# Scores of the first three query blocks with the keys held in 128x32 tiles and turned back by VectorE

## The reference

```python
q = jnp.concatenate([q_nope, apply_rope(q_rope)], axis=-1)
...
scores = jnp.einsum('bqhd,bkhd->bhqk', q, k) * scale
mask = jnp.tril(jnp.ones((S, S), dtype=bool))
scores = jnp.where(mask, scores, jnp.finfo(scores.dtype).min)
attn = jax.nn.softmax(scores, axis=-1)
out = jnp.einsum('bhqk,bkhd->bqhd', attn, v).reshape(B, S, N_HEADS * V_DIM)
return out @ Wo
```

## Time and profile before

| | us |
|---|---|
| median of 3 runs | 819.32 (818.69 to 820.13) |
| the profiled execution | 820.57 |
| its span from first to last instruction | 818.7 |
| TensorE busy | 800.7 (98%) |
| VectorE busy | 666.7 (81%) |
| ScalarE busy | 522.1 (64%) |
| GpSimd busy | 468.0 (57%) |

### The profile page before, as it was taken

How to read it: one execution, slowest core, us unless ns; L and a number is a source line. 1 busy time by engine, 2 the same in 40 slices (tenths; PEclk the granted TensorE clock), 3 DMA queues, 4 the chain that set the end, 5 groups by cost and what they waited for, 6 DMA issues and landing times.

```text
span 818.7 us, 22149 instructions
## 1 busy us (share of the span) xinstructions
PE 800.7 (98%) x7528; PEld 738.5 (90%) x7528; DVE 666.7 (81%) x2509; ACT 522.1 (64%) x1612; POOL 468.0 (57%) x1245
## 2 busy tenths in 40 slices
PE   7999999999999999999999999999999999999988
PEld 5988999888889899999999999999999999999967
DVE  6798787887687888988778887888888878897875
ACT  4554454454654787767767677677766767677582
POOL 6833022112335686676766667676676766667653
PEclk9999999999999999999999999999999999999999
DMA  8610012000001223221222312223221222212210
GB/s 303 232 34 1 1 65 66 1 1 1 1 14 33 55 45 59 49 53 35 45 48 51 62 33 47 40 45 59 45 53 35 45 49 51 59 33 48 41 40 28
DMA packets 101329, 41.09 MB, mean 50 GB/s; under 512 B 91744, under 2 KB 98400, under 8 KB 100576
## 3 DMA queue, kind: packets, MB, share of 16 engines
q1 hardware_dynamic: 98896, 38.89, 20.6%
q10 hardware_dynamic: 2320, 0.79, 0.4%
HBM read 14.47 MB, written 4.19 MB: 23 GB/s over the span
## 4 chain that ended last, share of the span: by engine, by line
PE 89%; DVE 4%; issue 2%; ACT 2%; POOL 2%; DMA 1%; ACTq 0%; POOLq 0%; DVEq 0%
PE bank L494 59%; PE bank L686 17%; PE bank L708 8%; PE bank L558 1%; POOL par L1727 1%; PE bank L568 1%; PE bank L608 1%; PE bank L511 1%; DVE QA L1492 1%; DVE PT L1526 1%; ACT SM L975 1%; DVE SM L1504 1%; PE bank L582 0%; DMA QT<-QA 0%; PE bank L633 0%
## 5 line engine op out<-in xcount | busy, mean ns | idle before, releaser
L1888 POOL TENSOR_SCALAR SM<-SM,stb 128x32 f32<-128x32 f32 (+7 forms) x512 | 195.1, 400 | 95.5 <-DVE stb L1511 91.9
L975 ACT ACTIVATE SM<-SM,stb 128x32 f32<-128x32 f32 (+7 forms) x512 | 206.1, 404 | 61.8 <-DVE stb L1504 58.1
L686 PE MATMUL bank<-KT,QT 128*128 128x192 f32 (+7 forms) x1024 | 166.9, 306 | 5.0 <-DVE stb L1504 4.8
L1504 DVE CUSTOM_DVE_ANT_0 SM<-bank,CONST 128x32 f32<-128x32 f32 (+7 forms) x512 | 126.7, 298 | 35.2 <-PE bank L686 32.4
L686 PEld LDWEIGHTS bank<-KT,QT 128*128 128x128 f32 x1024 | 147.0, 190 | 9.2 <-DVE stb L1504 5.9
L494 PE MATMUL bank<-yh,wq_lo 128*128 128x256 f32 x512 | 148.1, 289 | 0.2 <-DVE QA L1492 0.2
L494 PE MATMUL bank<-yl,wq_hi 128*128 128x256 f32 x512 | 144.2, 282 | 0.0
L494 PE MATMUL bank<-yh,wq_hi 128*128 128x256 f32 x512 | 144.1, 282 | 0.0
L1526 DVE STREAM_TRANSPOSE PT<-SM 128x384 f32<-128x384 f32 (+3 forms) x256 | 115.7, 481 | 18.6 <-PE bank L708 18.6
L494 PEld LDWEIGHTS bank<-yh,wq_lo 128*128 128x128 f32 x512 | 96.7, 189 | 0.4 <-DVE QA L1492 0.4
L494 PEld LDWEIGHTS bank<-yl,wq_hi 128*128 128x128 f32 x512 | 96.5, 189 | 0.0
(11 more groups left out here) (210 smaller groups left out, 1957.3 us busy)
## 6 DMA issues: line engine op xcount, KB each, us to landing
QT<-QA SPq DMA_DIRECT2D x248, 64.0 KB, 2.2
PT<-KV SPq DMA_DIRECT2D x256, 16.0 KB, 1.8
out<-fo SPq DMA_DIRECT2D x32, 128.0 KB, 2.0
X<-in_x SPq DMA_DIRECT2D x7, 512.0 KB, 11.6
stage<-in_wqn SPq DMA_DIRECT2D x2, 1024.0 KB, 9.7
stage<-in_wo SPq DMA_DIRECT2D x2, 1024.0 KB, 5.0
stage<-in_w1t SPq DMA_DIRECT2D x4, 256.0 KB, 5.7
stage<-in_w2t SPq DMA_DIRECT2D x2, 512.0 KB, 6.8
```

Of the source, the lines that this page charges most:

```text
L686: i = e.matmul(sbank[n % 2][:, at], Q[:, p, q, :, :].rearrange("p h c -> p (h c)"), KT[b % 3][:, p, 0:32 * q + 32], start=True, stop=True)
L975: i = e.activation(M[:, at], M[:, at], ACT.Exp, bias=S[:, 0, j:j + 1], scale=-1.0, accum_out=S[:, 1, j:j + 1])
L1504: i = e.tensor_tensor_reduce(M[:, at], bk[:, at], mask[:, 224 - 32 * q:256], 1.0, 3e38, ALU.add, ALU.min, S[:, 0, j:j + 1])
L1888: i = e.tensor_scalar(P[:, at], P[:, at], S[:, 2, j:j + 1], 1.0, ALU.mult, ALU.mult)
```

## The change

It cuts the units in another way. The wide units stay (`"W"`). A middle unit (`"M"`) has blocks 3, 4 and 5 of one group: 128, 160 and 192 columns. Blocks 0, 1 and 2 go into two units of a new kind (`"T"`), one for each p, with both halves in it. The count of units, of minima and of exponentials in a batch stays the same: 4 x 2 + 4 x 3 + 2 x 6 = 32, before 4 x 2 + 4 x 4 + 2 x 4.

In a T unit the operands change places: the keys of one block of 32 are stationary, in a tile of 128 rows by 32 columns, one such tile for each of the four heads of a group, and the queries of both halves move through it (192, 128 and 64 columns for key block 0, 1 and 2). These are 12 matmuls, 24 records. The scores come out with keys on the partitions, so `most(n)` first turns them with three transposes from PSUM into `SM`, waits for them on a semaphore of its own (`st`), and then takes six fused minima from `SM` in place. `turn_weights` has a branch for T units with three transposes, or four where the two halves stand in the buffers in reverse (5 of 16 batches).

The two T units stand at places 5 and 6, and `with_next` makes TensorE issue both in step 5, directly after the latents' sum. `QT` becomes one tensor with the three buffers in it, so that one access can read two halves. By place the kinds are now W, M, M, W, M, T, T, M, W, W; in the last batch M, M, T, T, M, M, W, W, W, W. `HALF_DONE` for half 0 goes from 5 to 7.

```diff
-ORDER = (0, 3, 2, 4, 1, 7, 8, 9, 6, 5)
+ORDER = (("W", 0, 0), ("M", 0, 1), ("M", 0, 0), ("W", 0, 1), ("M", 1, 0),
+         ("T", None, 0), ("T", None, 1), ("M", 1, 1), ("W", 1, 1), ("W", 1, 0))
...
+def with_next(n):
+
+    return n < TOTAL - 1 and unit(n)[1] == unit(n + 1)[1] == "T"
...
             def l1_s(n):
...
+                if kind == "T":
+
+                    at = 0
+                    Q = QT[:, both_halves(b), p, :, :, :]
+                    for kb in range(3):
+                        to = at + 64 * (3 - kb)
+                        for i in range(4):
+                            j = e.matmul(sbank[n % 2][32 * i:32 * i + 32, at:to],
+                                         KT[b % 3][:, p, 32 * kb:32 * kb + 32], Q[:, :, kb:3, i, :],
+                                         start=True, stop=True)
+                        at = to
...
-                if n < TOTAL:
+                if n < TOTAL and not (n and with_next(n - 1)):
                     l1_s(n)
+                    if with_next(n):
+                        l1_s(n + 1)
...
             def most(n):
...
+                if unit(n)[1] == "T":
+                    at = 0
+                    for kb in range(3):
+                        to = at + 64 * (3 - kb)
+                        i = e.transpose(early(M)[:, :, 3 * kb:5 + kb:2, :],
+                                        bk[:, at:to].rearrange("p (h q c) -> p h q c", h=2, c=32))
+                        at = to
+                    i.then_inc(SEM["st"], 1)
+                    turned_scores[0] += 1
+                    w.wait_ge("st", turned_scores[0])
+                    bk = M
...
             def turn_weights(n):
...
+                else:
+                    for q in range(3):
+                        i = e.transpose(PT[:, p:p + 3:2, 0:q + 1, q, :],
+                                        early(M)[:, :, 2 * q:3 * q + 1, :])
```

More of the change, by code:

```diff
@@ L92, in unit @@
     b, m = divmod(n, UNITS)
[L93 to L98, removed]
-def tiles(n):
-    return [(p, q, slice(at, at + 32 * q + 32)) for p, q, at in unit(n)[2]]
+    return b, *(LAST_ORDER if b == NB - 1 else ORDER)[m]
+def tiles(n):
+    kind = unit(n)[1]
+    if kind == "T":
+        at = [(q, EARLY * e + 64 * q) for e in range(2) for q in range(3)]
+    else:
+        at = [(6, 0), (7, 256)] if kind == "W" else [(3, 0), (4, 128), (5, 320)]
+    return [(q, slice(i, i + 32 * q + 32)) for q, i in at]
+def with_next(n):
+    return n < TOTAL - 1 and unit(n)[1] == unit(n + 1)[1] == "T"
 def shared_bank_order():
@@ L380, in qt_free, with both_halves @@
                 w.wait_ge("s", UNITS * ((n - 3) // 2) + HALF_DONE[(n - 3) % 2])
+        def both_halves(b):
+            first, second = sorted((2 * b + h) % 3 for h in range(2))
+            return slice(first, second + 1, second - first)
         def place(e, w, b, h, heads=range(4)):
@@ L674, in l1_s @@
             def l1_s(n):
-                b, h, _ = unit(n)
+                b, kind, half, p = unit(n)
+                halves = range(2) if half is None else (half,)
                 w.wait_ge("kt", b + 1)
-                for g in range(2):
-                    w.wait_ge("qn", n_nth[4 * b + 2 * h + g])
-                w.wait_ge(*moved(2 * b + h))
+                for h in halves:
+                    for g in range(2):
+                        w.wait_ge("qn", n_nth[4 * b + 2 * h + g])
+                    w.wait_ge(*moved(2 * b + h))
                 if n < 2:
@@ L683, in l1_s @@
                 w.wait_ge("mx", n - 1)
[L684 to L688, removed]
+                if kind == "T":
+                    at = 0
[7 more added lines that the diff above has]
+                        at = to
+                else:
+                    Q = QT[:, (2 * b + half) % 3, p, :, :, :]
+                    for q, at in tiles(n):
+                        j = e.matmul(sbank[n % 2][:, at], Q[:, q, :, :].rearrange("p h c -> p (h c)"),
+                                     KT[b % 3][:, p, 0:32 * q + 32], start=True, stop=True)
+                j.then_inc(SEM["s"], 1)
             def l1_pv(b, blocks, units):
@@ L973, in exps @@
                 w.wait_ge("mx", n + 1)
-                for j, (_, _, at) in enumerate(tiles(n)):
+                for j, (_, at) in enumerate(tiles(n)):
                     i = e.activation(M[:, at], M[:, at], ACT.Exp, bias=S[:, 0, j:j + 1], scale=-1.0,
@@ L1513, in turn_weights @@
             def turn_weights(n):
-                b, h, pairs = unit(n)
+                b, kind, h, p = unit(n)
+                M = SM[n % 5]
                 w.wait_ge("n", n + 1)
@@ L1521, in turn_weights, with turn @@
                     w.wait_ge("pv", b)
[L1522 to L1526, removed]
+                def turn(slot, q, at, k, some=2):
+                    src = M[:, at:at + 32 * some * k].rearrange("p (q k c) -> p q k c", q=some, c=32)
+                    return e.transpose(PT[:, slot, 0:k, q:q + some, :].rearrange("p k q c -> p q k c"), src)
+                if kind == "W":
+                    i = turn(2 * h + p, 6, 0, 8)
+                elif kind == "M":
+                    turn(2 * h + p, 3, 0, 4, 1)
+                    i = turn(2 * h + p, 4, 128, 6)
+                elif 2 * b % 3 == 2:
+                    for e_ in range(2):
+                        turn(2 - 2 * e_ + p, 0, EARLY * e_, 2)
+                        i = turn(2 - 2 * e_ + p, 2, EARLY * e_ + 128, 3, 1)
+                else:
+                    for q in range(3):
+                        i = e.transpose(PT[:, p:p + 3:2, 0:q + 1, q, :],
+                                        early(M)[:, :, 2 * q:3 * q + 1, :])
                 i.then_inc(SEM["pt"], 1)
```

28 lines of the change are left out of this document (16 added, 12 removed).

## The result

The changed kernel takes **822.11 us** (median of 19 runs, 820.57 to 824.58), the kernel before 819.35 (19 runs, 818.69 to 822.24): a ratio of 1.003, 95% interval 1.0022 to 1.0038. It is 2.8 us slower; 5.5 were forecast. The profiled run is the fastest of the 19, with the same span as before, 818.7 us. So the two profiles are compared here by stages and not by their spans. The scores are now L713 (middle and wide units) and L706 (T units), the projections L507, the latents' sum L735, the minima L1550, the score transposes L1542 and the turns L1572.

The account below looks back on a forecast made before the run. TensorE, busy without a gap in the steady part, was taken as the bound. Steady batches 3.9, batch 0 1.1 and the last batch 0.5 us sum to 5.5 on 819.32: 824.8 us, range 822 to 828 (chance 0.63).

Parts of the forecast that it names:

- The named wait: TensorE idles 0.8 us before the second T unit, until VectorE's minima M(4) are ready, in 14 batches.
- Rival (b): Faster: M(4) comes before the first T unit ends, no wait; a batch 0.65 us shorter, about 810 us; chance 0.05.
- M of a T unit: VectorE's transposes, wait and six minima for one T unit: 1.65 us where 0.83 was.
- the steady part: Batches with a sum ahead of the T units: each 0.28 us longer, 14 x 0.28 = 3.9 us.
- the ends: First and last batch: +1.1 us and +0.5 us.
- Removed from TensorE: New middle units of 0.81 us at places 1 and 2 save 2 x 0.15 = 0.30 us a batch; other places nothing.
- the second T unit: On TensorE after the wait: 0.10 restart, 0.75 work, 0.11 to leave the tiles; the projection ends 0.58 us later.
- rival (c): No change: T unit, restart and exit at their lower bounds, 14 x 0 and half of the ends, 820 us; chance 0.12.
- the price used ahead: 1.69 ns a column on TensorE, from a wide unit's 480 columns; a T unit's 384 columns take 0.65 us.
- batch 0: The projection now comes behind the wait for M(4): +1.5 us, less 0.3 to 0.4 for shorter units before, +1.1.
- The last batch: VectorE sets the pace: M(2) as a T unit +0.8 us, M(4)'s exponentials -0.3; together +0.5.

## Why the prediction came out as it did

**Right: direction and the wait.** The named wait was there, 14 times, 0.81 us (0.8 forecast) and twice 1.16, ended by M(4), with M(4) behind the turn that waits for the sum. Both cures removed it. Rival (b) had 810 for that; 810.2 was measured with the units apart, and 806.3, better than it, with M(4) ahead. M of a T unit is 1.67 us (1.65), and TensorE waits for it only in the last batch (1.41 us before S(4)), as forecast.

The time that came out, 822.11, lies in the forecast range partly by luck: the steady part was forecast too long and the ends too short, and the two errors offset each other in part.

**Wrong: the size of what the units save.** The step that failed is "Removed from TensorE", 0.30 us a batch. Its "thus 0.81 us" for the new middle unit came from a wide unit's start-to-start distance. But that mark moves with the shape of the last record: to the first record of the next projection it is 0.68 us (506.21 - 505.53), and that projection's second record is late, 0.26 behind its first, against 0.21 before:

```profile
506.93 0.28 PE L494 MATMUL bank<-yl,wq_hi 128*128 128x256 f32 x1
```

Counted to the second record, the old middle unit had 1.16 us and the new one has 0.94: **0.22 saved and not 0.15**. The old third kind had 1.01 and saves 0.07 where I had nothing, at place 7 and once more over places 3 and 4 together. Sum 2 x 0.22 + 2 x 0.07 = 0.58 us a batch instead of 0.30.

**Wrong, smaller: the second T unit.** The forecast had 0.10 to restart, 0.75 and 0.11 to leave. It measured 0.79 (517.55 - 516.76), which is 0.68 and 0.11. The restart cost nothing visible, and the 64-column group hid its loads. So the turn L621 starts 0.44 later behind the sum than the old one, (519.09 - 515.09) - (519.14 - 515.58), and not 0.58.

**Not foreseen:** the records of the products with 256 columns follow each other at 0.1190 us instead of 0.1185 (means over the steady part). All kernels that have the new units, with narrow tiles or without, lie at 0.1188 to 0.1190. In the changed kernel it comes to 0.07 us a batch. The cause is open.

The steady sum by the measured terms: +0.44 - 0.58 + 0.07 = -0.07 us a batch, and the two waits of 1.16 add 0.05 on average, so -0.02; measured -0.05. Forecast was +0.28. This is the "no change" of rival (c) for the steady part, by other terms than it gave.

**Too small: batch 0.** Forecast "+1.5, less 0.3 to 0.4". The pairing cost 1.75 (39.71 - 37.96), and the shorter units gave nothing: with T units apart, batch 0 takes 37.84 to 37.96 us against 37.75. At full clock VectorE and GpSimd set the pace there and not TensorE, as the chain shows. So it is +1.96 and not +1.1. The half clock behind the wait belongs to it. Its own share is known only for the order with the units apart in batch 0, 0.1 us. The last batch has +0.7 (0.5 forecast).

A rule against the row: the Trainium skill, "TensorE: Matmul & The Clock Gate", section "Part 3: Packing small matmuls — row/col tiling", gives 2.38 times for three column tiles of 32. Here four strips move 384 columns in 0.68 us against 0.65 for the columns alone by the price used ahead, so nearly the whole factor of four; the row decides. On the change of tiles, the Trainium skill, "TensorEngine Tiling (Array Packing)", section "Tiling Modes", says that it drains the array. The traces agree that it costs: 0.11 us from T tiles to a projection. The place counts as well: it is 0.32 us a batch more with T tiles between a projection and the transposes. How much of this is the change of tiles isn't shown.

## What to carry to other kernels

When a short unit takes the place of a long one, ask whose lateness the long one covered: here a projection of 1.5 us hid a VectorE result that was 0.8 late, and swapping two VectorE steps turned a loss of 3 us into a gain of 13. Price a unit up to the second record of what follows it, since the first record's start depends on the last shape before it. Price a wait by the distance from start to start as well: the 0.81 us in the list were 1.01 us of time. Before a step is moved, follow all that it issues on the other engines: the same reorder of TensorE was 4 us slower or 9 us faster than before, by whether its followers moved along, and the longest new wait was then for a buffer that was still being read.

## What the runs showed of the hardware that I had not expected

- Four 128x32 tiles with 192, 128 and 64 columns run side by side at about the columns' own pace (0.65 us): a unit of 24 records takes 0.68 us, and two take 1.45 up to the projection behind them. The same products in 128x128 tiles take 1.35 us a unit.
- TensorE's clock went to 1.2 GHz for 3.4 us and more within 1.4 us of the end of idle stretches of 1.73, 1.98, 2.06, 2.25, 2.97 and 3.58 us, and did not behind others of 1.93, 1.97, 2.21 and 2.25. Length alone doesn't decide it in these traces. The price ran from 0.1 us in a batch 0 where VectorE and GpSimd were nearly as late, to 1.8 on one latents' sum.
- The waits of 1.16 us instead of 0.81 fall on batches 1 and 10 of the changed kernel, where the turn behind the sum starts 0.35 us late. In batch 1 it does so in the kernel before as well, in batch 10 not. The cause is open.
